# Score and maxima matmuls of an attention read 64 partitions of their row tile, the unused ones zeroed once per buffer

## The reference, cut to what matters

```python
# block 1: softmax over all keys, then the upper triangle is kept
p = jax.nn.softmax(q @ k.T / sqrt(s)); z = (p * triu) @ v
# blocks 2 and 3: causal
scores = jnp.where(causal, q @ k.T * scale, min); attn = softmax(scores) @ v
```

## Time and profile before

| | us |
|---|---|
| median of three runs | 3361.97 |
| lowest and highest | 3353.67, 3379.85 |
| the profiled execution's own time | 3366.61 |
| its span, first to last instruction | 3364.9 |
| TensorE (PE) busy | 2913.9 (87%) |
| VectorE (DVE) busy | 1972.5 (59%) |
| ScalarE (ACT) busy | 1435.5 (43%) |
| GpSimd (POOL) busy | 360.0 (11%) |
| granted TensorE clock, mean of the span | 0.733 |

### The profile page before, as it was taken

One profiled execution on the slowest core, in us unless ns is written; L12 is line 12 of the kernel. 1 busy time (PEld: TensorE's weight loads), 2 busy tenths in 40 slices (PEclk: granted clock), 3 DMA queues, 4 the chain that ended last, 5 costly groups with the idle time before them and its releaser, 6 DMA issues. The chain is left out here.

```text
span 3364.9 us, 40017 instructions
## 1 busy us (share of the span) xinstructions
PE 2913.9 (87%) x14544; PEld 1293.3 (38%) x14544; DVE 1972.5 (59%) x3987; ACT 1435.5 (43%) x2105; POOL 360.0 (11%) x544
## 2 busy tenths in 40 slices
PE   4799999999645999999859849999999598979897
PEld 2333334333213433443334324333433245634563
DVE  3698898986155654665245447645654265535554
ACT  1177676765411345344512203454345324632463
POOL 1000001000010000100100010001000133303330
PEclk8599999997765555555569965555555698988898
DMA  5000000000020000000000020000000012301230
GB/s 197 23 22 8 20 9 22 10 7 2 18 75 39 14 18 11 26 9 5 6 14 0 0 77 22 7 20 31 6 8 3 30 38 91 104 18 38 86 109 18
DMA packets 73403, 106.03 MB, mean 32 GB/s; under 512 B 23704, under 2 KB 46232, under 8 KB 71576
## 3 DMA queue, kind: packets, MB, share of 16 engines
q1 hardware_dynamic: 69856, 92.15, 8.1%
q10 hardware_dynamic: 3384, 11.74, 0.9%
HBM read 51.17 MB, written 17.17 MB: 20 GB/s over the span
## 5 line engine op out<-in xcount | busy, mean ns | idle before, releaser
L684 ACT ACTIVATE att_probs<-psum 128x1024 f32<-128x1024 f32 (+3 forms) x1152 | 1039.2, 951 | 1029.0 <-PE psum L728 1028.5
L637 DVE TENSOR_REDUCE att_part_max<-psum 128x1 f32<-128x512 f32 x1792 | 1133.2, 683 | 397.9 <-PE psum L710 396.8
L710 PE MATMUL psum<-att_k_rows,att_q_rows 34*128 34x512 f32 (+3 forms) x2304 | 982.3, 602 | 132.0 <-DMA att_k_rows<-att_ones 63.1
L710 PEld LDWEIGHTS psum<-att_k_rows,att_q_rows 34*128 34x128 f32 x2304 | 464.8, 252 | 971.0 <-DVE att_part_max L637 575.7
L753 PE MATMUL psum<-att_probs,v_aug 128*9 128x512 f32 (+3 forms) x3712 | 648.7, 786 | 15.6 <-ACT att_z_sb L676 15.6
L728 PE MATMUL psum<-att_q_rows,att_k_rows 34*128 34x512 f32 (+3 forms) x2304 | 564.6, 511 | 12.2 <-DMA att_q_rows<-att_max_rows 8.8
L634 DVE CUSTOM_DVE_ANT_0 att_masked<-psum,mask_max_sb 128x384 bf16<-128x384 f32 (+3 forms) x512 | 235.4, 486 | 261.6 <-PE psum L710 260.3
L728 PEld LDWEIGHTS psum<-att_q_rows,att_k_rows 34*128 34x128 f32 x2304 | 341.9, 264 | 93.7 <-ACT att_probs L684 47.4
L590 POOL TENSOR_SCALAR_AFFINE_SELECT att_probs<-att_probs 128x256 f32<-128x256 f32 x256 | 102.9, 408 | 1242.7 <-ACT att_probs L684 1240.5
L1334 ACT ACTIVATE latt_probs<-psum,latt_bias,latt_scale 128x192 f32<-128x192 f32 x256 | 127.5, 507 | 122.2 <-DVE latt_bias L1373 122.2
L749 PE MATMUL psum<-att_probs,att_one_only 128*9 128x512 f32 (+3 forms) x1280 | 158.5, 569 | 10.6 <-ACT att_z_sb L676 10.5
(11 more groups left out here) (254 smaller groups left out, 2549.9 us busy)
## 6 DMA issues: line engine op xcount, KB each, us to landing
att_k_rows<-k_pieces SPq DMA_DIRECT2D x48, 256.0 KB
latt_k<-local_k_T SPq DMA_DIRECT2D x32, 384.0 KB, 3.0
att_q_rows<-q_pieces SPq DMA_DIRECT2D x168, 64.0 KB
lproj_table<-in_tables SPq DMA_DIRECT2D x16, 512.0 KB, 3.6
latt_q<-local_q_T SPq DMA_DIRECT2D x32, 256.0 KB, 2.4
latt_v_own<-local_v_tok SPq DMA_DIRECT2D x32, 256.0 KB, 2.3
k_pieces<-proj_piece SPq DMA_DIRECT2D x12, 512.0 KB, 2.8
q_pieces<-proj_piece SPq DMA_DIRECT2D x12, 512.0 KB, 2.7
```

The costliest lines, as they stand in the source:

```text
L637: nc.vector.tensor_reduce(column, ring[e % NRING][:, 0:w], AX.X, ALU.max).then_inc(ring_free, 1)
L684: nc.scalar.activation(probs[s % NPROBS][:, pr, :, at:BANK], st[pr][:, :, at:BANK], ACT.Exp, scale=scale).then_inc(st_free, 1)
L710: nc.tensor.matmul(ring[e % NRING][:, 0:w], q_rows[u % NQ][rows, pr, qt * P:(qt + 1) * P].bitcast(F32R), k_rows[g % 2][rows, pr, kc * BANK ...
```

## The change

`ROWS` becomes 64. Partitions 32 to 63 of each row tile are set to zero once in each buffer of `q_rows` and `k_rows` at the start of each attention, by VectorE for the buffers used first and by GpSimd for the others; after that the two extra rows are overwritten as before, and the other 30 stay zero. The writes of zeros into the two extra rows of `q_rows` are left out for the first use of each buffer (units 0 to 3), since the memsets cover them, and the waits follow. `set_ones(0)` waits for the memsets of `k_rows[0]`, `set_ones(1)` for all of GpSimd's.

```diff
--- before.py
+++ after.py
@@ -25,9 +25,10 @@
 NPIECE = 3
 HIGH = -4096
 PROD = 4 * HD
-ROWS = PROD + 2
+ROWS = 2 * PROD
 NG = 4
 NQ = 4
+NK = 2
 NRING = 3
 BEHIND = 6
 SPARE = 10
@@ -480,6 +481,8 @@
         m_in = [sem(f"m_in{b}") for b in range(NQ)]
         z_out = [sem(f"z_out{b}") for b in range(2)]
         fill_set = sem("fill_set")
+        rows_clear = sem("rows_clear")
+        more_clear = sem("more_clear")
         ones_in = [sem(f"ones_in{b}") for b in range(2)]
         zeros_in = [sem(f"zeros_in{b}") for b in range(NQ)]
         z_clear = sem("z_clear")
@@ -496,6 +499,7 @@
         z_free = sem("z_free")
         z_in = sem("z_in")
         QIN, KIN, MIN_, ZOUT = 16 * 4, 16 * 4, 16 * 2, 16 * 4
+        MORE = 2 * (NQ - 2 + NK - 1)
         diagonals = [s for s, (u, kb) in enumerate(steps) if plan.on_diagonal(u, kb)]
         diag_number = {s: n for n, s in enumerate(diagonals)}
         block = ctx.enter_context(nc.Block())
@@ -545,17 +549,17 @@
 
             load_k(0)
             sp.wait_ge(fill_set, 2)
+            sp.wait_ge(rows_clear, 2)
             set_ones(0)
             load_q(2)
-            zero_max(2)
             put_max(0)
             load_q(3)
-            zero_max(3)
             for u, (g, c) in enumerate(units):
                 if u + 1 < NU:
                     put_max(u + 1)
                 if u == 0:
                     load_k(1)
+                    sp.wait_ge(more_clear, MORE)
                     set_ones(1)
                 if u > 0:
                     store_z(u - 1)
@@ -580,6 +584,13 @@
 
         @block.gpsimd
         def _(pool):
+            for i in range(2):
+                spare = slice(64 * i + PROD, 64 * i + ROWS)
+                for b in range(2, NQ):
+                    nc.gpsimd.memset(q_rows[b][spare, :, :], 0.0).then_inc(more_clear, 1)
+                for b in range(1, NK):
+                    nc.gpsimd.memset(k_rows[b][spare, :, :], 0.0).then_inc(more_clear, 1)
+            pool.wait_ge(more_clear, MORE)
             for s, (u, kb) in enumerate(steps):
                 if plan.on_diagonal(u, kb):
                     at = kb % 4 * P
@@ -599,6 +610,13 @@
 
         @block.vector
         def _(dve):
+            for i in range(2):
+                spare = slice(64 * i + PROD, 64 * i + ROWS)
+                nc.vector.memset(k_rows[0][spare, :, :], 0.0).then_inc(rows_clear, 1)
+            for i in range(2):
+                spare = slice(64 * i + PROD, 64 * i + ROWS)
+                for b in range(2):
+                    nc.vector.memset(q_rows[b][spare, :, :], 0.0).then_inc(rows_clear, 1)
             nc.vector.memset(zeros[:, :], 0.0).then_inc(fill_set, 1)
             nc.vector.memset(ones[:, :], 1.0).then_inc(fill_set, 1)
             nc.vector.memset(z_ps[:, :], 0.0).then_inc(z_clear, 1)
@@ -663,11 +681,6 @@
                         piece = q_dram[a, c].rearrange("(g i d p) s -> g i d (p s)", g=NG, i=2, p=2)[g, i]
                         act.dma_start(q_rows[u][rows, :, :].rearrange("r p s -> r (p s)"),
                                       piece.unsqueeze(0).to_broadcast([2, HD, 2 * BANK])).then_inc(q_in[u], 16)
-                if u == 0:
-                    act.wait_ge(fill_set, 1)
-                for i in range(2):
-                    row = 64 * i + PROD
-                    act.dma_start(q_rows[u][row:row + 2, :, :].rearrange("n p s -> n (p s)"), zeros[:, :]).then_inc(zeros_in[u], 16)
 
             def take_z(u):
                 act.wait_ge(pv_done, plan.first_step[u + 1])
@@ -699,7 +712,12 @@
                         g, c = units[u]
                         if e == plan.begun_at[u]:
                             pe.wait_ge(q_in[u % NQ], QIN * (u // NQ + 1))
-                            pe.wait_ge(zeros_in[u % NQ], 32 * (u // NQ + 1))
+                            if u == 0:
+                                pe.wait_ge(rows_clear, 6)
+                            if u == 2:
+                                pe.wait_ge(more_clear, MORE)
+                            if u >= NQ:
+                                pe.wait_ge(zeros_in[u % NQ], 32 * (u // NQ))
                             if u == 0 or units[u - 1][0] != g:
                                 pe.wait_ge(k_in[g % 2], KIN * (g // 2 + 1))
                                 pe.wait_ge(ones_in[g % 2], 32)
```

## The result

The changed kernel takes 3020.36 us (median of four runs, 3009.75 to 3024.06) where the kernel before took 3360.97 (median of four, 3353.67 to 3379.85); the ratio is 0.8974, with a 95% interval of 0.8931 to 0.9017. The prediction was 3025, faster with a chance of 0.85.

What follows compares the result with a forecast made beforehand. TensorE's clock was taken to bound the causal attentions, 2 x 626 of 3365 us. Savings of 310 + 18.6 + 5 + 4 = 337.6 us took the profiled 3366.6 to 3029, 3025 for the median; range 2955 to 3160.

Steps and rivals of the forecast that it cites:

- What bounds the kernel, and that rows count: Causal attentions: bound by TensorE's clock, 0.51 at 0.97 busy; how much of the array works raises it, not busy time.
- nothing changes: Rival, whole kernel: clock answers to busy time or to rows carrying data; 3362 us less up to 4, chance 0.12.
- At an equal clock 64 rows cost nothing: Maxima and scores: 4608 matmuls going from 34 to 64 rows take the same time at an equal clock.
- The causal attentions: Second and third attention: clock up for most of the time, 155 us saved in each, 310 in both.
- the deductions: Each causal attention: 13.6, 6.5, 6.6 and 5 us taken back, 31.7 off the 186.6 saved at full clock throughout.
- the piece that I gave nothing: Second attention, 1341.5 to 1384.9 us: shortest units leave the array half idle, so no gain, 13.6 us taken back.
- The wait behind the load of k: Causal attentions: wait of 3.0 us for the maxima's rows behind `load_k`, to grow by 5.
- The first attention: Its end: 18.6 us saved in the last unit but one, 5 in the last; middle stays VectorE's.
- the slower one: Rival, first attention: more rows taken as load, clock cut; 3622 us if all 14 units slow, chance 0.03.
- the half case: Rival, causal attentions: clock rises only in the widest units and falls between; 3157 us for the median, chance 0.13.
- Memsets: Each attention's start: 10.6 us on VectorE, 10.5 or 30.4 on GpSimd, all taken as hidden, costing nothing.
- Fewer writes of zeros: Eight small DMAs fewer per attention, shortening unit 1's wait: 4 us for all three attentions, bounds 0 and 6.

## Why the prediction was right, step by step

The mechanism was right; that the sum came within 5 us of the median was luck in part, since terms that were off in both directions cancelled.

**What bounds the kernel, and that rows count.** Right, and shown: 34 rows with everything else of the change gives the old time, 40, 48 and 64 rows give less and less, and either kind of matmul serves. The contrast of equally busy windows pointed at the cause. The rival "nothing changes" falls with its two grounds: busy time alone is not what the clock answers to, and zeros count like numbers (3025 with zeros replaced). (Its time stands as 3363 in one place and 3362 in another; the sum gives 3362.) The rule of the Trainium skill on gaps ("TensorE: Matmul & The Clock Gate", section "Why this matters for your kernels"), which the prediction weighed, is not enough to forecast this kernel: TensorE's gaps are fewer at 34 rows (busy 0.97) than at 64 (0.92), and yet the clock stays at 0.51 with 34.

**At an equal clock 64 rows cost nothing.** Right. From 115 to 140 us only maxima run, at 0.50; the group of TensorE's matmuls there by form, before and after:

```profile
L710 PE MATMUL psum<-att_k_rows,att_q_rows 34*128 34x512 f32 x43 | 25.9, 791 | 0.0
```

```profile
L728 PE MATMUL psum<-att_k_rows,att_q_rows 64*128 64x512 f32 x44 | 26.5, 791 | 0.0
```

791 ns each, with 34 rows and with 64. The first attention's middle keeps its pace too, 614.40 us for 4297 records against 629.80 for 4377, and a unit takes 45 us in both; but there VectorE sets the pace, so it shows less.

**The causal attentions.** 155 us forecast for each, 161.8 and 168.9 measured in the stretches of the earlier trace rows. By the pieces of the earlier trace rows, what I forecast with the deductions and what came: 99.3 and 94.4; 43.1 and 41.6; 70.0 and 75.7; 43.4 and 33.5; 87.2 and 86.4; 43.1 and 41.5; 85.3 and 91.4. In all 471.4 and 464.5. VectorE's share where it sets the pace was 0.893 against the 0.891 assumed. Two terms were off and nearly cancelled. ScalarE's share where it leads came out at 58.82 / 75.7 = 0.78 and 71.07 / 91.4 = 0.78, not 0.85; I had put it near that of a stretch without maxima, where TensorE has no other work to put between the scores (whether that is the reason was not tested). Nor does ScalarE bound these pieces by itself: in the first of them it stood idle 17.3 us for TensorE's scores, and TensorE was busy 70.44 of the 75.7 us, where I had counted half of 114.94. Which of the two sets the pace there stays open. And the piece that I gave nothing (43.4) fell to 33.5: its clock reached 0.81. The short units do lose the clock for part of their time, but they were also waiting for TensorE at 1.2 GHz, which I had denied them.

**The wait behind the load of k.** I let it grow by 5; it grew from 3.02 to 6.32, so by 3.3, and the unit that holds it took 42.4 us where the one without it takes 35.3. Delaying the load removed it.

**The first attention.** This term failed, and it hid. I counted 18.6 us for its last unit but one and 5 for the last. The profiles seemed to confirm it (-21.9), but the kernels with 34 rows there take 763.3 and 764.2 us against 757.4: 6 to 7 us by the profiles, and 2 to 6 by the medians. Of these some 4 us are the last unit's, about as estimated. The rest, the 18.6, was in the one profiled execution that I worked from. I had read one unit's low clock as a property of 34 rows; fourteen units at 1.00 before it should have told me that a second execution need not have it.

**The rivals.** The clock did not fall in the first attention (1.00 over 614.40 us), so nothing came of the slower one; nor did it swing in the widest units (1.00 over the fourth unit), which the half case had asked for.

**Memsets.** 0.83 ns an element was right: 3.47 us for 4,096 and 0.91 for 1,024 on VectorE. With gaps between them they took 12.4 us rather than 10.6 and delayed the ones to 88.3 (forecast about 89). I took nothing for them, and they cost 1.9 us in each attention, 5.7 in all; the first maxima came at 106.7, between the 105 to 106 that I had called right and the 108 that I had called wrong. GpSimd's took 3.50 and 0.92 us, the lower of my two bounds.

**Fewer writes of zeros.** 4 us forecast; from the first maxima to the first transpose (L716 before) the causal attentions take 10.0 us each where they took 13.2 and 13.0, the wait of unit 1 being gone: 6.2 us, slightly over my upper bound of 6, and about what the memsets cost.

**The untouched rest.** Not in the sum, and it cost 10 us of the profile: 743.6 against 733.6. The clock fell there once more than before. Windows of 17 us from about the same point of a projection with 32-row and 128-row matmuls, before and after (at the lower clock fewer records fit into the same 17 us):

```profile
2765.00:2782.00 17.00, 17.00 (x43) 5.61 (x42) 10.11 (x17) 4.85 (x9) 6.08 (x5) 1.00 0.10 31
```

```profile
2409.00:2426.00 17.00, 17.00 (x19) 5.09 (x19) 4.24 (x9) 2.39 (x4) 0.48 (x1) 0.50 0.11 31
```

In the profiles of the twelve other kernels this rest takes 730.6 to 740.1 us, so its length changes from execution to execution without any edit to it. The prediction landed 5 us from the median with a first attention counted too high by about 17, a rest that scatters by 13, and causal attentions counted too low by 21.

## What to carry to other kernels

Where TensorE is busy without gaps and its clock is still at the lower level, look at how much of the array the matmuls use, and compare windows of equal busy time with other shapes: unused rows of a row tile that are filled with zeros and read along are free in time and can bring the clock up. Near the edge a few rows decide, and what is gained is bounded by the next engine, here VectorE at 0.89 of the time; where it doesn't lead, the pieces stopped with ScalarE at 0.78 and TensorE busy 0.91 to 0.93, and no run shows which bounds them. Don't build a term on a low stretch that occurs once in one execution: the clock moves between executions of the same program.

## What the runs showed of the hardware that I had not expected

- At 0.50 a maxima matmul takes 791 ns with 34 rows and with 64.
- Half of the added rows bring 0.84 to 0.88 of the gain (3061 to 3074 us, of 3359 to 3020), and 40 rows 0.31.
- Rows count in steps smaller than 8 (34 and 40 rows: 3359 and 3253 us) and zeros like constants that are not zero (3020 and 3025), while 32 columns instead of 9 in the products bring no clock at all (0.51).
- VectorE's and GpSimd's memsets of 32 x 4,096 elements ran side by side at 3.47 and 3.50 us, neither slowed: with VectorE idle GpSimd's took 3.51 in the kernel with the memsets shared out.
- A projection that no edit touches, with 32-row matmuls among 128-row ones, ran 17 us at 0.50 in one execution and at 1.00 in another.
- Splitting the load of q as that of k was split, which spread it over more engines, delayed the start by 5.5 to 5.8 us in each attention instead of bringing it forward.
